# Graph attention on one core: another order of a step's short operations on VectorE and of TensorE's products

## The reference

```python
def _gat_layer(x, src, dst, W, a_s, a_d, b):
    h = (x @ W).reshape(n, HEADS, C)
    s_src = jnp.einsum('nhc,hc->nh', h, a_s)
    s_dst = jnp.einsum('nhc,hc->nh', h, a_d)
    e = jax.nn.leaky_relu(s_src[src] + s_dst[dst], NEG_SLOPE)
    m = jax.ops.segment_max(e, dst, num_segments=n)
    ex = jnp.exp(e - m[dst])
    denom = jax.ops.segment_sum(ex, dst, num_segments=n)
    alpha = ex / denom[dst]
    msg = h[src] * alpha[:, :, None]
    out = jax.ops.segment_sum(msg, dst, num_segments=n)
    return out.reshape(n, HEADS * C) + b
```

## Time and profile before

| | |
|---|---|
| median of 3 runs | 8613.78 us (8613.48 to 8619.50) |
| profiled execution, its own time | 8616.01 us |
| its span | 8614.3 us |
| mean granted PE clock | 0.892 |
| busy in the span: PE, DVE, ACT, POOL | 5772.8, 5314.5, 3000.2, 5327.6 us |
| graph attention's messages (L2263), first to last | 6221.1 to 8553.1 us, 366 of them |
| busy of L2218, L2263 (DVE) | 862.4, 446.3 us |
| busy of L2186 (POOL) | 1591.2 us |
| busy of L2338, L2339, L2355 (PE) | 499.1, 569.8, 727.7 us |

### The profile page before, as it was taken

One profiled execution on the slowest core, in us unless ns is written; L12 is line 12 of the kernel. 1 busy time (PEld: TensorE's weight loads), 2 busy tenths in 40 slices (PEclk: granted clock), 3 DMA queues, 4 the chain that ended last, 5 costly groups with the idle time before them and its releaser, 6 DMA issues. The chain is left out here.

```text
span 8614.3 us, 153149 instructions
## 1 busy us (share of the span) xinstructions
PE 5772.8 (67%) x32873; PEld 4638.9 (54%) x33057; DVE 5314.5 (62%) x15225; ACT 3000.2 (35%) x7461; POOL 5327.6 (62%) x5323
## 2 busy tenths in 40 slices
PE   0003445535555955997997998798488878887885
PEld 0003435534345844775775776677366656665664
DVE  8002336664442227776776776776688868886887
ACT  0000100000011213443443444444366646655664
POOL 1777777757713124775775776677277747765774
PEclk9997767767877977998999999999799989998998
DMA  1401123333317952445445445444233433343334
GB/s 70 161 2 36 52 62 101 101 77 104 104 28 251 371 189 71 105 105 89 105 105 91 105 105 88 107 105 99 58 96 94 91 74 94 95 80 87 94 94 71
DMA packets 597319, 865.53 MB, mean 100 GB/s; under 512 B 273716, under 2 KB 411446, under 8 KB 595807
## 3 DMA queue, kind: packets, MB, share of 16 engines
q0 software_dynamic: 233280, 595.84, 29.1%
q1 hardware_dynamic: 363934, 268.70, 10.3%
HBM read 740.80 MB, written 125.29 MB: 101 GB/s over the span
## 5 line engine op out<-in xcount | busy, mean ns | idle before, releaser
L1743 POOL DMA_INDIRECT hs<-tab_agnn,rec x1952 | 1910.2, 979 | 723.6 <-issue 542.7
L2186 POOL DMA_INDIRECT hs<-tab_gat,rec x1464 | 1591.2, 1087 | 622.4 <-issue 425.8
L1809 DVE CUSTOM_DVE_ANT_0 prod<-psG,hs 128x256 f32<-128x256 f32 x1952 | 828.8, 480 | 505.8 <-DMA hs<-tab_agnn,rec 410.2
L1872 PE MATMUL psG<-HN,ohT 128*128 x3904 | 977.3, 392 | 41.8 <-DVE lg L1809 34.7
L2218 DVE TENSOR_REDUCE mt<-psL 128x2 f32<-128x1024 f32 x732 | 862.4, 1217 | 162.2 <-PE psL L2339 103.3
L1889 PE MATMUL psV<-hs,pr 128*128 128x258 f32 x3904 | 937.4, 384 | 0.0
L1826 ACT ACTIVATE prT<-cand,mn 128x512 f32<-128x512 f32 x488 | 352.4, 722 | 1261.6 <-DVE mn L1769 1247.7
L1872 PEld LDWEIGHTS psG<-HN,ohT 128*128 128x128 f32 x3904 | 707.3, 192 | 151.8 <-DVE lg L1809 51.3
L1889 PEld LDWEIGHTS psV<-hs,pr 128*128 128x128 f32 x3904 | 709.6, 192 | 82.5
L2355 PE MATMUL psV<-msg,oh 128*128 128x260 f32 x2928 | 727.7, 393 | 1.7 <-DVE msg L2263 1.4
L782 PE MATMUL psT<-ident,oh 128*128 128x128 f32 x416 | 100.6, 388 | 915.5 <-DVE oh L747 915.5
(11 more groups left out here) (342 smaller groups left out, 12084.4 us busy)
## 6 DMA issues: line engine op xcount, KB each, us to landing
w<-in_L_gnn_w SPq DMA_DIRECT2D x224, 512.0 KB, 5.6
hs<-tab_agnn,rec POOLq DMA_INDIRECT x1952
fwd_d<-acc SPq DMA_DIRECT2D x10, 2730.0 KB
fw<-fwd_d SPq DMA_DIRECT2D x104, 260.0 KB, 2.8
hs<-tab_gat,rec POOLq DMA_INDIRECT x1464
rec<-rec_d SPq DMA_DIRECT2D x1166, 10.0 KB, 1.8
b<-in_L_gnn_b SPq DMA_DIRECT2D x113, 128.0 KB, 6.4
x<-xbuf SPq DMA_DIRECT2D x112, 128.0 KB, 5.9
```

What stands on the lines that cost most here:

```text
L1743: nc.gpsimd.indirect_dma_start(out=hs[:, j, g, :], out_offset=None, in_=k.tab_agnn, in_offset=bass.IndirectOffsetOnAxis(ap=rec[:, j, g, 0: ...
L1809: ins = V.tensor_tensor_reduce(prod[:, h2, g, :], psG[:, bank(j2, half), m, :], hs[:, j2, g, 0:D], hs[:, j2, g, D:D + 1], 0.0, ALU.mult, A ...
L1872: mm = nc.tensor.matmul(psG[:, bank(j1, half), m, :], ohT[:, j1 % 2, 2 * half + m, :], pick(HN, b, slice(None)).rearrange("p a c -> p (a c ...
L2186: nc.gpsimd.indirect_dma_start(out=hs[:, j, g, :], out_offset=None, in_=k.tab_gat, in_offset=bass.IndirectOffsetOnAxis(ap=rec[:, j, g, 0:1 ...
```

## The change

On DVE the logits' add (L2235) moves up behind the reductions, the part of leaky that belongs to the edges stands behind the scaling of `acc`, then `smax`, `t3`, the second `raw`, the clip, the add of `psV` and the product. Leaky of the block's part is an instruction of its own (one more per step), and it and `df` now stand behind the product, at the step's end. The waits follow their instructions, and the count of `s_leak` is two a step. On PE the messages' product (L2355) moves from between the two pairs to the front of the step.

```diff
--- before.py
+++ after.py
@@ -2150,7 +2150,6 @@
 
                     pairs = lambda t: layer * (NG * 2) + t * 2
                     spread = lambda t: layer * (NG * 2) + (L2_LAYERS * NG + t * 2)
-                    step_of = lambda t: layer * (NG + 1) + t
 
                     def at_block(v, b):
                         return pick(v, b, slice(None)).rearrange("p a h -> p (a h)")
@@ -2219,50 +2218,50 @@
 
                             top(0)
                             top(1)
+                            if old:
+                                dve.wait_ge(q.q, own(t) + 1)
+                                V.tensor_tensor(g3(raw, now), hrow[:, :, :, C_HEAD], q3[:, :, 0, :], ALU.add).then_inc(s_lg, 1)
                             if add:
                                 dve.wait_ge(q.rs, flow(t6) + 1)
                                 if not (isinstance(t6, int) and t6 < 1):
                                     dve.wait_ge(q.u, added(t6))
                                 a4 = acc.rearrange("p (h c) -> p h c", h=HEADS)
                                 V.tensor_tensor(a4, a4, b3(rs[:, j6, :], CH1), ALU.mult).then_inc(s_am, 1)
+                            if old:
+                                dve.wait_ge(s_lg, own(t) + 1)
+                                V.scalar_tensor_tensor(out=leaky[:, now, 0:GH], in0=raw[:, now, 0:GH], scalar=NEG_SLOPE,
+                                                       in1=raw[:, now, 0:GH], op0=ALU.mult, op1=ALU.max).then_inc(s_leak, 1)
                             if mid_:
                                 dve.wait_ge(s_lt, pairs(t2) + 2)
                                 V.tensor_tensor(at_block(smax, b), at_block(smax, b), mt[:, h2, :], ALU.max).then_inc(s_mx, 1)
+                            if old:
+                                dve.wait_ge(s_leak, pairs(t) + 2)
+                                V.tensor_tensor(g3(t3, h), g3(leaky, now), q3[:, :, 1, :], ALU.subtract).then_inc(s_t3, 1)
+                            if mid_:
                                 dve.wait_ge(s_mx, own(t2) * 2 + 1)
                                 V.tensor_tensor(raw[:, now, GH:], at_block(smax, b), at_block(sd, b), ALU.add).then_inc(s_mx, 1)
-                            if old:
-                                dve.wait_ge(q.q, own(t) + 1)
-                                V.tensor_tensor(g3(raw, now), hrow[:, :, :, C_HEAD], q3[:, :, 0, :], ALU.add).then_inc(s_lg, 1)
-                            if mid_ or old:
-                                if old:
-                                    dve.wait_ge(s_lg, own(t) + 1)
-                                if mid_:
-                                    dve.wait_ge(s_mx, own(t2) * 2 + 2)
-                                    if not (isinstance(t2, int) and t2 < 1):
-                                        dve.wait_ge(q.m, flow(t2))
-                                part = slice(0 if old else GH, GH + HEADS if mid_ else GH)
-                                V.scalar_tensor_tensor(out=leaky[:, now, part], in0=raw[:, now, part], scalar=NEG_SLOPE,
-                                                       in1=raw[:, now, part], op0=ALU.mult, op1=ALU.max).then_inc(s_leak, 1)
-                            if old:
-                                dve.wait_ge(s_leak, step_of(t + 1) + 1)
-                                V.tensor_tensor(g3(t3, h), g3(leaky, now), q3[:, :, 1, :], ALU.subtract).then_inc(s_t3, 1)
-                            if mid_:
-                                dve.wait_ge(s_leak, step_of(t2) + 1)
-                                if not (isinstance(t2, int) and t2 < 2):
-                                    dve.wait_ge(q.rs, flow(t2 - 1))
-                                V.tensor_tensor(df[:, h2, :], at_block(peak, b), leaky[:, now, GH:], ALU.subtract).then_inc(q.df, 1)
                             if old:
                                 dve.wait_ge(s_t3, own(t) + 1)
                                 V.tensor_scalar(t3[:, h, :], t3[:, h, :], 60.0, None, ALU.min).then_inc(q.tt, 1)
                             if add:
+                                dve.wait_ge(s_am, own(t6) + 1)
                                 dve.wait_ge(q.v, nth(t6) + 1)
-                                dve.wait_ge(s_am, own(t6) + 1)
                                 V.tensor_tensor(acc, acc, psV[:, j6 % 2, 0:W_GAT], ALU.add).then_inc(q.u, 1)
                             if old:
                                 dve.wait_ge(q.e, flow(t) + 1)
                                 V.tensor_tensor(hmsg[:, :, :, 0:C_HEAD], hrow[:, :, :, 0:C_HEAD],
                                                 hmsg[:, :, :, C_HEAD].unsqueeze(3).to_broadcast([P, G, HEADS, C_HEAD]),
                                                 ALU.mult).then_inc(q.msg3, 1)
+                            if mid_:
+                                if not (isinstance(t2, int) and t2 < 1):
+                                    dve.wait_ge(q.m, flow(t2))
+                                dve.wait_ge(s_mx, own(t2) * 2 + 2)
+                                V.scalar_tensor_tensor(out=leaky[:, now, GH:], in0=raw[:, now, GH:], scalar=NEG_SLOPE,
+                                                       in1=raw[:, now, GH:], op0=ALU.mult, op1=ALU.max).then_inc(s_leak, 1)
+                                if not (isinstance(t2, int) and t2 < 2):
+                                    dve.wait_ge(q.rs, flow(t2 - 1))
+                                dve.wait_ge(s_leak, pairs(t2) + 1)
+                                V.tensor_tensor(df[:, h2, :], at_block(peak, b), leaky[:, now, GH:], ALU.subtract).then_inc(q.df, 1)
                         pipeline(dve, step, 6, numbers=blocks)
 
                     @block.scalar
@@ -2321,6 +2320,17 @@
 
                         def step(i, j):
                             last, mid_, low, add = (lagged(i, j, n) for n in (1, 2, 3, 5))
+                            if add:
+                                _, j5, t5 = add
+                                h5 = j5 % 2
+                                pe.wait_ge(q.msg3, own(t5) + 1)
+                                pe.wait_ge(q.oh, nth(t5) + 1)
+                                if not (isinstance(t5, int) and t5 < 2):
+                                    pe.wait_ge(q.u, added(t5 - 1))
+                                for g in range(G):
+                                    mm = nc.tensor.matmul(psV[:, h5, 0:W_GAT], oh[:, h5, g, :], msg[:, h5, g, :],
+                                                          start=(g == 0), stop=(g == G - 1))
+                                mm.then_inc(q.v, 1)
                             if last:
                                 i1, j1, t1 = last
                                 pe.wait_ge(s_away, own(t1) + 1)
@@ -2344,18 +2354,6 @@
                                 pe.wait_ge(s_st, own(t2) + 1)
                                 pe.wait_ge(q.ev, flow(t2) + 1)
                                 pair(0)
-                            if add:
-                                _, j5, t5 = add
-                                h5 = j5 % 2
-                                pe.wait_ge(q.msg3, own(t5) + 1)
-                                pe.wait_ge(q.oh, nth(t5) + 1)
-                                if not (isinstance(t5, int) and t5 < 2):
-                                    pe.wait_ge(q.u, added(t5 - 1))
-                                for g in range(G):
-                                    mm = nc.tensor.matmul(psV[:, h5, 0:W_GAT], oh[:, h5, g, :], msg[:, h5, g, :],
-                                                          start=(g == 0), stop=(g == G - 1))
-                                mm.then_inc(q.v, 1)
-                            if mid_:
                                 pair(1)
                             if low:
                                 _, j3, t3_ = low
```

## The result

| | before | changed |
|---|---|---|
| median (13 runs each) | 8613.48 us (8607.02 to 8619.50) | 8634.40 us (8628.31 to 8638.65) |
| ratio, 95% interval | | 1.0024 (1.0016 to 1.0033) |
| profiled execution, own time | 8616.01 us | 8637.06 us |
| a layer's exponentials, first to last | 718.0, 716.4, 716.1 us | 724.9, 726.1, 724.2 us |
| six steps (median over the loops) | 35.45 us | 35.84 us |

The change costs 20.9 us, 0.24%. In the profiled pair the three layers' loops are 24.8 us longer, 57 turns of +0.39 us being 22 of them, and the rest of the program some 4 us shorter.

A forecast was written before the change was run, and what follows sets the result against it. It took DVE's timeline as the bound before, and the ring through ACT as setting the changed ordinary step; per turn -0.14 + 0.62 + 0.08 = +0.56, over 57 turns +32 us, 8646 us against the median, range 8598 to 8690.

The forecast's parts named there:

- ring: Ordinary step: exponential, product, leaky, df, ACT's copy, evictions, next exponential; sum 5.64, between 5.5 and 5.7, setting the step.
- the edge: Turn's end: df holds DVE's queue, so block-number loads lie uncovered; 7.54 against 6.92, a loss of 0.62, bounds 7.34 to 7.75.
- Rivals 1 and 3: 1: loads stay under the product at the edge, 8574, chance 0.12; 3: DVE's 5.32 sets the step, 8555, chance 0.06.
- ordinary steps: The turn's five steps away from its edge: 28.4 against 28.54, a gain of 0.14 per turn.
- rival 2: ACT's ring is shorter by 0.13, 5.52 a step: 8609, no change that can be told; chance 0.24.
- The two places that no row of before showed: In ACT's ring: df to L2301, taken 0.39 (0.31 to 0.31 + 0.12); L2290 to exponential, taken 0.52 (0.48 to 0.61).
- 5.24 to 5.35: Ordinary step by the DVE path alone, from exponential through df, reduction and clip to the next exponential.
- 0.08 behind the edge: Step behind the turn's edge: DVE is late, so the add L2260 sets the product, 0.08 more per turn.
- hold-ups: Small delays of DVE's instruction queue, 0.39 over five ordinary steps; half (0.2) kept, the rest falling in DVE's slack of 0.3.
- Fill and drain: Start and end of the group loops, claimed to keep their cost.
- Costed at nothing: PE's new order: waits about 0.6 for L2301 before psQ, priced at nothing with 0.6 of cover.
- Rival 4: PE's longer idle before psQ at the edge lowers its clock: at least 1 us a turn, 57 more, 8703; chance 0.08.

The follow-up runs named there:

- act_order: Changed kernel with ACT's copy of the peak and rs moved behind the three evictions of PSUM; ratio 1.0048 to the kernel before.
- ring_fixed: mid_before with leaky and df put behind the product in each turn's last step only; ratio 0.9907 to the kernel before.
- edge_fixed: Changed kernel with the block's leaky and df ahead of the product in each turn's last step; 8594.35 us, ratio 0.9980 to the kernel before.
- pe_only: Kernel before with PE's new order alone; 8608.99 us against 8614.05, ratio 0.9995.
- dve_only: Changed kernel with PE's old order, leaving DVE's new order; 8642.39 us, ratio 1.0034 to the kernel before.
- act_edge: act_order with edge_fixed's last step, leaky and df ahead of the product there; ratio 0.9912 to the kernel before.
- mid_before: Changed kernel with the block's leaky and df ahead of the product in all steps; 8456.05 us, ratio 0.9815 to the kernel before.

## Why the prediction was right, point by point

**Direction and mechanism.** Forecast slower, 8646 us (8598 to 8690); measured 8634. The loss came the way it was told: two short operations behind the product close a ring through ACT and uncover the loads at the edge. Rivals 1 and 3 would have shown edges of 6.3 or ordinary steps of 5.3, rival 2 ordinary steps of 5.52; the trace has 7.49 and 5.63.

**The ring.** Forecast 5.64, measured 5.63 to 5.64. Its terms: exponential to product 0.24 (0.26), product to leaky 1.14 (1.13), leaky to df 0.31 (0.30), df to copy 0.38 (0.39), copy to L2289 3.04 (3.04), on to the exponential 0.52 (0.52). The two places that no row of before showed were taken well, and that was partly luck. With the lowest values that the prediction allowed there, 0.31 and 0.48, its own rival 2 would have been the forecast, no change; with the highest, 0.43 and 0.61, the sum is 5.77, above the 5.7 that it gives as the upper end. act_order shows that the step is this ring's, and DVE's own queue then needs 5.44, 0.1 more than the 5.24 to 5.35 of the prediction: df to reduction is 0.28, not 0.15.

**The edge.** Forecast 7.54, measured 7.49; df to reduction 2.33 against 2.25. That the queue is held fits every edge looked at: the arithmetic of the loop starts with the last operation of the turn, with df at 7256.9 here and at 7333.8 in ring_fixed, with the product at 7265.7 in edge_fixed. By the Trainium skill (Perfetto Trace Analysis, DVE / Act Engine Instruction) the sequencer is free once an instruction has gone into the hardware wait queue. The arithmetic could then have started under the product, from 7255.42; this trace disagrees.

**The size.** Forecast +0.56 a turn, measured +0.39, hence 21 us and not 32. The mis-sized term is that of the ordinary steps. I had five of them at 28.4 plus 0.08 behind the edge, 0.06 less than before; by the medians of six steps and of the edge they are 35.84 - 7.49 = 28.35 against 35.45 - 6.93 = 28.52, 0.17 less. With ACT late, DVE's hold-ups disappear in its slack almost entirely; only the step behind the edge, 5.80, shows one. The edge gave +0.56 for +0.62. Fill and drain, held at nothing, gave the loops' other 2.6 us, and the rest of the program ran some 4 us shorter in that pair, which no step of mine covers.

**PE.** Costed at nothing, and pe_only and dve_only bear it out within their intervals. Rival 4's mechanism is real, but it costs next to nothing in the changed kernel. PE idles there around the edge as well, and the next sum can run at the lower clock, as its timeline shows:

```profile
7257.60 1.05 PE L2365 MATMUL psQ<-sp,ohT 128*128 x8 [0.55 <-ACT sp L2300]
7259.25 3.20 PE L2331 MATMUL psV<-msg,oh 128*128 128x260 f32 x8 [0.60 <-issue]
```

3.20 us for a sum that takes 2.00; the granted clock is 0.50 from 7261 to 7263. In every second turn the idle time before psQ reaches 1.9 to 2.0 us in the step behind the edge, near the 2 that the prediction named. The clock falls at the edge or in the two intervals behind it in 30 of the 57 turns, against 23 in the kernel before, and only 4 of the second intervals are over 6 us. So the fall is mostly hidden; that the slack of the long edge hides it is my reading, not tested by itself. In act_order the same fall came in 55 of 57 turns and was no longer hidden, and cost about 1.2 us a turn, its second interval against act_edge's. The price that rival 4 named, at least 1 us a turn, was about right; its cover was thicker than thought. In mid_before the clock falls there in 3 turns of 57.

## What to carry to other kernels

Put short operations between long ones by the readers they have on other engines, not by the room: an operation that another in-order engine waits for belongs ahead of the long one, and with a stranger between it and the result it reads. Before a loop's edge keep a long operation last, already handed over, so that the register loads run under it; a short last operation that has to wait for a result uncovers them. Whether a short one without such a wait would do so too was not tried. And price a longer idle gap of PE by who reads PE's next products: the clock behind it may have fallen.

## What was not expected of the hardware

The clip, 128 x 16 numbers, usually takes 0.16 us. In mid_before it takes more than twice as long in most steps (the step shown above is one of the others, with 0.17). The view by line of the changed kernel and of mid_before (ns min/median/max):

```profile
L2245 DVE TENSOR_SCALAR t<-t x366: 159/163/383, 6216.7 to 8573.7; 128x16 f32<-128x16 f32 x183
```

```profile
L2245 DVE TENSOR_SCALAR t<-t x366: 166/377/387, 6217.0 to 8395.5; 128x16 f32<-128x16 f32 x183
```

The median is 377 against 163 ns for the same instruction, while its successor starts 0.21 behind it in the long cases and in the short ones. The exponential, which waits for its end, comes 0.41 and not 0.20 behind its start. What holds the end back was not tried. It costs an ordinary step of mid_before little: the product starts 0.87 behind the clip in the mean in the long cases, 0.93 in the short ones.
